# The diagonal products of a state-space scan in four column quarters of the array instead of two halves

## The chip, the cores and the metric

The kernel runs on one core of one Trainium2 chip. A core has TensorE (PE in the profile, with its weight loads listed apart as PEld), VectorE (DVE), ScalarE (ACT), GpSimd (POOL) and SyncE (SP, which issues most DMAs). The metric is the device time of one execution in microseconds, lower is better; times are medians of several runs.

## The reference

A batch of 32 sequences of 512 tokens and 256 channels goes through one block: a layer norm, a projection with rotary embedding, a gated state-space layer (scan) with 8 heads of 64 channels and a state of 128, an output projection, and then a mixture of experts (a shared part and 16 small experts, four of them chosen per token). The change touches one term of the scan:

```python
Acs = jnp.cumsum(Adt, axis=-1)
Lmat = jnp.exp(segsum(Adt))
Y_diag = jnp.einsum('bcln,bcsn,bhcls,bcshp->bclhp', Cr, Br, Lmat, xdt)
...
Y_off = jnp.einsum('bcln,bchpn,bhcl->bclhp', Cr, states_prev, jnp.exp(Acs))
return (Y_diag + Y_off).reshape(b, l, h, p)
```

`Y_diag` is the part of a token's output that comes from tokens of its own chunk. `l` is the query token, `s` the key token, `h` the head, `p` the channel in the head. Everything is float32.

## The kernel before

The kernel makes its own chunks of 128 tokens, four per sequence. For a chunk `c` and a head `h`, the decay times `C.B` stands in the tile `seg` as a matrix of 128 key tokens (partitions) by 128 query tokens, and the inputs in `xdt` as 128 key tokens by 64 channels of each of 8 heads. `diagonal(c)` (from L1567 of the source; its matmuls carry the line L1577 in the profile) multiplies them into one PSUM bank of the group `apb`: query tokens on partitions, 8 x 64 channels along the row. The stationary operand (the weights that are loaded) is a piece of `seg`, the moving operand the 64 columns of `xdt` that belong to the head. The loop over `n` cuts the 128 query tokens into two halves of 64, so each product uses 64 of the array's 128 columns, and the half's place in the PSUM partitions (0 or 64) is the column half of the array that it uses. That makes 16 matmuls for a chunk. A float32 matmul shows in the trace as two passes, each a weight load and a matmul record, so a chunk shows 32 loads and 32 matmuls. Over 32 sequences of 4 chunks there are 128 such chunks, 4096 records of each kind.

Large projections (helper `split_mm`, line L1443) run in another type (fp32r) with the operands split into a high and a low part, three products for one; their weights have 128 columns. Transposes have the lines L1452 and L1462, the state products L1560 and L1567 (float32, 512 moving columns, two passes), the router's L1492 and L1494 (16 or 32 moving columns), the products of B and C L1547, the cumulated decays L1518 to L1520 (the last with a weight of 32 columns), the down projection of the experts L1631.

Each engine runs one instruction list written out by hand. PE's is `lead`, `first`, `iteration(False)`, then a hardware loop of 29 repeats of `iteration`, then `tail`, `drain`, `last`. In `iteration` the work of three sequences is interleaved: the scan of one, the expert layer of the one before, the input projection of the next. The four `diagonal` calls stand between projections, each after others' work; PE waits for `m_ready` (DVE has multiplied `seg`, L1167) and for a free bank, and gives the bank to DVE's `chunk_y` (L1191, L1193). At the head of each repeat PE waits at L1530 for `hTl`, which DVE makes last in the repeat before. The loop's own jump has the line L1735.

Of the kernel before, what the change touches and what calls it, by code (L numbers as in the profile page):

```python
# [12 lines left out]
P = 128  # L13
# [19 lines left out]
def build(nc, x, wq_t, wzx_t, conv_w, conv_b, dt_bias, a_log, d_param, npw, ngw, wo_t,  # L33
# [6 lines left out]
    with ctx:  # L40
# [1366 lines left out]
        def _(pe):  # L1407
# [9 lines left out]
            def slot(name):  # L1417

                part, n = way.plan.where[name]
                w = len(BANKS[part])  # L1420
                if n >= w:
                    s, k = out_of(way.plan.slots[part][n - w][0], way.plan)
                    pe.wait_ge(sem[s], now(s, k) if SEM[s][3] else k)
                elif part != "p":
                    old = way.before if part in way.before.slots else way.plan
                    s, k = out_of([slot[0] for slot in old.slots[part][n::w]][-1], old)
                    pe.wait_ge(sem[s], k)
                return way.bank(name)

            def read_out(name):  # L1430
                s, k = out_of(name, way.plan)
                pe.wait_ge(sem[s], now(s, k) if SEM[s][3] else k)

            def fill(name, ins):
                part, n = way.plan.where[name]
                ins.then_inc(sem[f"{part}_for_{way.plan.slots[part][n][1]}"], 1)
# [132 lines left out]
            def diagonal(c):  # L1569
                b = slot(f"yd{c}")  # L1570
                read_out(f"xt{c}")
                pe.wait_ge(sem["m_ready"], c + 1)
                for h in range(HS):
                    hs = slice(h * PD, (h + 1) * PD)
                    for n in range(2):
                        ls = slice(n * P // 2, (n + 1) * P // 2)
                        ins = nc.tensor.matmul(b[ls, hs], seg[:, c % 2, h, ls], xdt[:, c % 2, hs], start=True, stop=True)  # L1577
                fill(f"yd{c}", ins)

# [81 lines left out]
            def first():  # L1661
                begin("first", "pa")
                consts(); weights_split(1, 2); project_z(0, 0); project_z(0, 1); project_z(1, 0)
                project_z(2, 0); project_z(1, 1); project_z(3, 0); project_x(4); project_x(5); project_x(0)
                project_z(2, 1); project_x(1); cumulate(); project_x(2); settled("ad_ready"); project_x(3)
                project_z(3, 1); x_by_token(0); CB(); x_by_token(1); B_by_token(); state(0); diagonal(0)
                state(1); from_state(1); diagonal(1); x_by_token(2); from_state(2); state(2); x_by_channel(0)
                y_by_channel(0); diagonal(2); x_by_token(3); weights_split(3); project_out(0)
                settled("a_out_ACT", "xdec_ready"); y_by_channel(1); project_q(0); project_out(1)
                from_state(3); y_by_channel(2); x_by_channel(1); diagonal(3); project_q(1); settled("xn_ready")  # L1670
                settled("m_ready"); project_out(2); settled("p_out_DVE"); y_by_channel(3); h_by_channel(0)
                project_out(3); settled("p_out_ACT"); settled("a_out_DVE", "yg_ready"); h_by_channel(1)
                settled("qn_ready")
                weights_split(*range(4, len(SPLIT)))
                assert not open_
# [117 lines left out]
```

## Time and profile before

| What | Value |
|---|---|
| Median of 3 runs | 3132.39 us (3128.45 to 3133.99) |
| The profiled execution's own time | 3137.47 us |
| Its span, first to last instruction | 3135.8 us |
| PE busy | 3058.7 us, 98% |
| PEld busy | 2624.5 us, 84% |
| DVE / POOL / ACT busy | 2360.5 / 2041.9 / 1934.2 us |
| The 29 repeats of the loop | about 94.4 to 94.9 us each |

The busy time of PE is that of records whose ends are modelled and which overlap, so it says that PE had work almost all the time, not how fast it went. For PE the distance from the start of one record to the start of the next of its kind is what is read. The pieces that the chain of waits gives to PE are such distances.

### The profile page before, as it was taken

The page shows a single profiled execution, that of the slowest core. Times are in us where ns is not written, and L with a number is a line of the kernel's source. Part 1 is how long each engine was busy: PE and PEld are TensorE (multiplying, and loading weights), DVE is VectorE, ACT ScalarE, POOL GpSimd, SP SyncE. Part 2 cuts the span into 40 slices and gives each one's busy share as a digit, 9 for nine tenths or more (in the row PEclk, how much of TensorE's full clock was granted, in tenths as well). Part 3 has the DMA queues.
Part 4 walks back from the last instruction along what each step waited for, and adds up shares of the span by engine and source line. Part 5 has one row for each costly group of instructions (what it writes and reads, how often), then busy time and mean ns, then how long its engine had stood idle before and what let it go on. Part 6 is the DMA issues. An engine that isn't in the chain of part 4 may idle for free.

```text
span 3135.8 us, 66479 instructions
## 1 busy us (share of the span) xinstructions
PE 3058.7 (98%) x21696; PEld 2624.5 (84%) x21696; DVE 2360.5 (75%) x5104; ACT 1934.2 (62%) x4149; POOL 2041.9 (65%) x2311
## 2 busy tenths in 40 slices
PE   5799999999999999999999999999999999999997
PEld 4688888888888888888888888888888888888876
DVE  5877877777777777777777777777777778777762
ACT  5566666666666566666666666666666666656562
POOL 2477666677666677666677666776666776666774
PEclk8899999999999999999999999999999999999998
DMA  3123222222222222222222222222222122222221
GB/s 125 41 69 89 74 76 66 67 67 88 74 65 69 70 72 81 78 68 61 73 78 78 81 67 58 67 87 78 78 66 62 67 88 74 81 61 67 68 82 41
DMA packets 143435, 227.37 MB, mean 73 GB/s; under 512 B 18976, under 2 KB 88352, under 8 KB 143392
## 3 DMA queue, kind: packets, MB, share of 16 engines
q1 hardware_dynamic: 126496, 210.06, 20.4%
q0 software_dynamic: 16896, 16.78, 4.1%
q8 instruction: 22, 0.36, 0.0%
q14 instruction: 21, 0.17, 0.0%
HBM read 174.87 MB, written 35.13 MB: 67 GB/s over the span
## 4 chain that ended last, share of the span: by engine, by line
PE 68%; POOL 24%; issue 2%; DMA 1%; DVE 1%; ACT 0%; POOLq 0%; SPq 0%; DVEq 0%; ACTq 0%
PE fpb L1443 25%; PE apb L1443 16%; PE acc L1631 13%; POOL hidL L652 5%; POOL hid L647 5%; POOL xD L622 3%; PE apb L1452 3%; PE apb L1577 2%; POOL zs L623 2%; PE apb L1567 2%; POOL rstd L583 1%; PE apb L1560 1%; PE ppb L1443 1%; POOL qrot L596 1%; POOL seg L607 1%
## 5 line engine op out<-in xcount | busy, mean ns | idle before, releaser
L652 POOL TENSOR_TENSOR hidL<-hid,hidH 128x512 fp32r<-128x512 f32 x384 | 546.2, 1422 | 239.3 <-ACT hidH L914 231.5
L1130 DVE SCALAR_TENSOR_TENSOR xc<-apb,cw,xc 128x511 f32<-128x511 f32 (+2 forms) x576 | 427.9, 747 | 70.3 <-ACT xc L827 42.1
L1631 PE MATMUL acc<-WDH,hidH 128*128 128x256 f32 x1536 | 458.2, 298 | 5.5 <-POOLq L654 4.7
L914 ACT CAST hidH<-hid 128x512 fp32r<-128x512 f32 x384 | 236.5, 616 | 368.2 <-POOL hid L647 310.2
L1631 PE MATMUL acc<-WDH,hidL 128*128 128x256 f32 x1536 | 432.3, 281 | 0.0
L1631 PE MATMUL acc<-WDL,hidH 128*128 128x256 f32 x1536 | 431.6, 281 | 0.0
L647 POOL TENSOR_TENSOR hid<-hid,cb 128x512 f32<-128x512 f32 x256 | 348.2, 1360 | 38.0 <-DMA cb<-c_row 13.4
L1249 DVE TENSOR_TENSOR hid<-hid,fpb 128x512 f32<-128x512 f32 x384 | 261.1, 680 | 142.4 <-PE fpb L1443 138.9
L1443 PE MATMUL fpb<-fTh,UH 128*128 128x512 f32 x768 | 336.4, 438 | 0.0
L1443 PE MATMUL fpb<-fTh,GH 128*128 128x512 f32 x768 | 319.5, 416 | 0.0
L845 ACT ACTIVATE seg<-seg,acs 128x128 f32<-128x128 f32 x1024 | 313.6, 389 | 8.9 <-ACT cb L895 5.7
L1631 PEld LDWEIGHTS acc<-WDH,hidH 128*128 128x128 f32 x1536 | 290.3, 189 | 26.7 <-POOLq L654 10.8
L1443 PE MATMUL fpb<-fTh,GL 128*128 128x512 f32 x768 | 304.8, 397 | 0.0
L1443 PE MATMUL fpb<-fTh,UL 128*128 128x512 f32 x768 | 303.8, 396 | 0.0
L1443 PE MATMUL fpb<-fTl,GH 128*128 128x512 f32 x768 | 303.7, 395 | 0.0
L1443 PE MATMUL fpb<-fTl,UH 128*128 128x512 f32 x768 | 302.5, 394 | 0.0
L1631 PEld LDWEIGHTS acc<-WDL,hidH 128*128 128x128 f32 x1536 | 290.8, 189 | 12.8 <-issue 7.2
L903 ACT ACTIVATE hid<-fpb 128x512 f32<-128x512 f32 x384 | 228.9, 596 | 115.5 <-PE fpb L1443 75.4
L1631 PEld LDWEIGHTS acc<-WDH,hidL 128*128 128x128 f32 x1536 | 290.2, 189 | 0.0
L622 POOL TENSOR_TENSOR xD<-xD,xdt 128x512 f32<-128x512 f32 x128 | 209.4, 1636 | 23.5 <-DVEq L1196 23.4
L827 ACT ACTIVATE xc<-apb,cbv,cw 128x512 f32<-128x512 f32 x192 | 149.2, 777 | 112.2 <-PE apb L1443 68.4
L1167 DVE TENSOR_TENSOR seg<-seg,CBs 128x1024 f32<-128x1024 f32 x128 | 166.0, 1297 | 43.1 <-ACT seg L845 33.6
(195 smaller groups left out, 8604.4 us busy)
## 6 DMA issues: line engine op xcount, KB each, us to landing
seg<-acs_row SPq DMA_DIRECT2D x128, 512.0 KB, 4.2
cb<-c_row SPq DMA_DIRECT2D x512, 128.0 KB, 2.9
xsP<-in_x SPq DMA_DIRECT2D x32, 512.0 KB, 3.7
xc<-qrot SPq DMA_DIRECT2D x32, 512.0 KB, 3.4
xc<-in_x SPq DMA_DIRECT2D x32, 512.0 KB, 4.4
out<-xc SPq DMA_DIRECT2D x32, 512.0 KB, 2.9
out<-xn POOLq DMA_DIRECT2D x32, 512.0 KB, 6.0
ZL_loaded<-in_wzx_t SPq DMA_DIRECT2D x2, 512.0 KB, 4.5
```

The lines of the kernel that those rows point to most:

```text
L622: own.do(G.tensor_tensor(xD[:, c % 2, :], xD[:, c % 2, :], xdt[:, c % 2, :], ALU.add))
L647: G.tensor_tensor(hid[:, j % 2, :], hid[:, j % 2, :], cb[:, r % 2, :], ALU.mult).then_inc(sem["routed_ready"], 1)
L652: own.do(G.tensor_tensor(hidL[:, j % 2, :], hid[:, j % 2, :], hidH[:, j % 2, :].bitcast(fp32), ALU.subtract))
L827: A.activation(xc[:, b, :], way.bank(f"xc{b}")[:], ACT.Identity, bias=cbv[:, b:b + 1], scale=cw[:, b, TAPS - 1:TAPS]).then_inc(sem["conv_f ...
L845: ins = A.activation(seg[:, c % 2, h, :], seg[:, c % 2, h, :], ACT.Exp, bias=acs[:, 0, c * HS + h:c * HS + h + 1])
L903: own.do(A.activation(hid[:, j % 2, :], way.bank(f"G{j}")[:], ACT.Silu))
L914: A.copy(hidH[:, j % 2, :], hid[:, j % 2, :]).then_inc(sem["hidden_high"], 1)
L1130: ins = V.scalar_tensor_tensor(xc[:, b, s:], src[:, 0:T - s], cw[:, b, TAPS - 1 - s:TAPS - s], xc[:, b, s:], ALU.mult, ALU.add)
L1167: V.tensor_tensor(seg[:, c % 2, :, :], seg[:, c % 2, :, :], CBs[:, c, :].unsqueeze(1).broadcast_to([P, HS, P]), ALU.mult).then_inc(sem["m_ ...
L1249: own.do(V.tensor_tensor(hid[:, j % 2, :], hid[:, j % 2, :], way.bank(f"U{j}")[:], ALU.mult))
L1443: ins = nc.tensor.matmul(dst, l, r, start=n == 0, stop=n == total - 1)
L1631: ins = nc.tensor.matmul(dst, l[:, w, tk], r[:, j, :], start=j == 0 and t % 2 == 0 and n == 0, stop=j == HB - 1 and n == 2, skip_group_che ...
```

## The change

The loop over halves becomes a loop over quarters of 32 query tokens. The moving operand stays at 64 columns, and the weights of one product have 32 columns instead of 64. A chunk has 32 matmuls instead of 16, in the trace 64 loads and 64 matmul records instead of 32, and each goes to one of four column quarters of the array (PSUM partitions 0, 32, 64, 96). Semaphores, banks and all other engines' lists are as before.

```diff
                 for h in range(HS):
                     hs = slice(h * PD, (h + 1) * PD)
-                    for n in range(2):
-                        ls = slice(n * P // 2, (n + 1) * P // 2)
+                    for n in range(4):
+                        ls = slice(n * P // 4, (n + 1) * P // 4)
                         ins = nc.tensor.matmul(b[ls, hs], seg[:, c % 2, h, ls], xdt[:, c % 2, hs], start=True, stop=True)
                 fill(f"yd{c}", ins)
```

On PE, at the first of the four chunks in the loop's repeat (`project_z(3, 1); diagonal(0); up(5)`), the list changes as follows (weights' columns x moving columns, then the count):

```order
 L1443 MATMUL apb<-ZL,hTh 128x256
 L1443 MATMUL apb<-ZH,hTl 128x256
-L1577 MATMUL apb<-xdt,seg 64x64 x16
+L1577 MATMUL apb<-xdt,seg 32x64 x32
 L1443 MATMUL fpb<-fTh,UH 128x512
 L1443 MATMUL fpb<-fTl,UH 128x512
```

Nothing else stands in another place: the block has twice as many instructions, between the same neighbours.

On PE, at the third chunk of the repeat (`up(7)`, `diagonal(2)`, then the transposes of `x_by_token(3)` and `down(5)`):

```order
 L1443 MATMUL fpb<-fTl,UH 128x512
 L1443 MATMUL fpb<-fTh,UL 128x512
-L1577 MATMUL apb<-xdt,seg 64x64 x16
+L1577 MATMUL apb<-xdt,seg 32x64 x32
 L1452 MATMUL apb<-ident,xc 128x128 x4
 L1631 MATMUL acc<-WDH,hidH 128x256
```

Here too the block grows in place. Counted in the built programs, one repeat of the loop on PE has 1,414 instructions before and 1,670 with the change, and the loop begins after 2,250 instructions before and after 2,762 with the change.

## Rows read from the trace of the kernel before

**Rows 1.** The page: engines' busy time, share of the span, and instructions.

```profile
PE 3058.7 (98%) x21696; PEld 2624.5 (84%) x21696; DVE 2360.5 (75%) x5104; ACT 1934.2 (62%) x4149; POOL 2041.9 (65%) x2311
```

**Rows 2.** Stretches: us, then each engine's busy us (instructions), granted clock, DMA share, GB/s.

```profile
174.00:2919.00 2745.00, 2742.86 (x19664) 2361.36 (x19663) 2117.32 (x4612) 1732.94 (x3742) 1846.92 (x2089) 1.00 0.25 73
1499.18:1594.03 94.85, 94.75 (x680) 81.43 (x679) 73.00 (x159) 59.83 (x130) 63.56 (x73) 1.00 0.24 72
```

**Rows 3.** Matmuls of L1577, all run: count, duration ns min/median/max, first and last start.

```profile
L1577 PE MATMUL apb<-xdt,seg x4096: 222/222/369, 70.4 to 3034.7; 128*64 128x64 f32 x196
```

**Rows 4.** Timeline of PE, 1504.5 to 1507: start us, us to its end, line, count.

```profile
1504.81 0.39 PE L1443 MATMUL fpb<-fTl,UH 128*128 128x512 f32 x1
1505.04 0.40 PE L1443 MATMUL fpb<-fTh,UL 128*128 128x512 f32 x1
1505.37 1.15 PE L1577 MATMUL apb<-xdt,seg 128*64 128x64 f32 x32
1506.45 0.66 PE L1452 MATMUL apb<-ident,xc 128*128 128x128 f32 x4
```

**Rows 5.** The same timeline in 1505.3 to 1505.42, the block's first records.

```profile
1505.37 0.14 PEld L1577 LDWEIGHTS apb<-xdt,seg 128*64 128x64 f32 x2 [0.37 <-issue]
1505.37 0.28 PE L1577 MATMUL apb<-xdt,seg 128*64 128x64 f32 x2
```

**Rows 6.** The chain of waits, 1640 to 1690: start us, us of the piece, line, count.

```profile
1644.44 0.10 PE fpb L1494
1644.55 0.12 PE fpb L1492
...
1667.24 0.89 PE apb L1547 x8
...
1671.37 0.44 PE apb L1452 x4
1671.81 0.44 PE fpb L1610 x4
...
1676.47 0.86 PE apb L1567 x2
```

**Rows 7.** Weight loads by line and form: count, busy us, mean ns, idle us before them.

```profile
L1577 PEld LDWEIGHTS apb<-xdt,seg 128*64 128x64 f32 x4096 | 130.4, 138 | 38.4 <-issue 34.3
...
L1567 PEld LDWEIGHTS apb<-xdec,Btok 128*128 128x128 f32 x192 | 36.2, 191 | 24.0 <-ACT zs L855 7.4 <-issue 6.9 <-DVE xD L1162 2.2
...
L1610 PEld LDWEIGHTS fpb<-ident,gt 128*16 128x16 f32 x128 | 11.4, 90 | 1.9
...
L1520 PEld LDWEIGHTS apb<-upper,ad 128*32 128x32 f32 x64 | 4.4, 108 | 1.3
```

**Rows 8.** DMA queues, 0 to 300 us: packets, MB, share of 16 engines.

```profile
q8 instruction: 14, 0.23, 0.3%
```

**Rows 9.** DMA queues, 300 to 2960 us (every queue that moved anything).

```profile
q1 hardware_dynamic: 103368, 178.51, 20.4%
q0 software_dynamic: 14784, 14.68, 4.2%
q14 instruction: 2, 0.02, 0.0%
```

**Rows 10.** The page: DMA queue 8 over the whole run, columns as in rows 8.

```profile
q8 instruction: 22, 0.36, 0.0%
```

**Rows 11.** PE's sequencer at the loop's jump: count, duration ns min/median/max, first and last start.

```profile
L1735 PEldq COMPARE_BRANCH  x29: 76/208/232, 306.3 to 2956.9; - x29
```

**Rows 12.** PE's sequencer at the first wait of a repeat, the same columns.

```profile
L1530 PEldq EVENT_SEMAPHORE  x32: 51/1968/2242, 34.2 to 2957.0; - x32
```

**Rows 13.** DMA issues by line, all run: count, size, median us from issue to landing.

```profile
acs_row<-acsT SPq DMA_DIRECT2D x32, 16.0 KB, 1.4
...
npwc<-in_npw SPq DMA_DIRECT2D x1, 1.0 KB, 3.1
...
ngwc<-in_ngw SPq DMA_DIRECT2D x1, 2.0 KB, 2.2
```

## The prediction

> **What bounds the kernel now.** I read the page's busy shares first [rows 1]: PE has work 98% of the span. Busy PE is not fast PE, so next the stretches [rows 2]: in the 2745 us that hold nearly all the repeats, PE is without work for 2.1 us, at a granted clock of 1.00 (the 2.4 GHz level), and the next busiest engine, DVE, is busy for 2117. One repeat takes 94.4 to 94.9 us and holds 680 matmul records and as many loads. So in the loop PE's own list sets the time. What PE's list gains or loses in a diagonal block moves the end by as much; other engines only follow, as they are released by PE. All that matters is how long PE stays in the block.
>
> The timeline of one block [rows 4] gives that. The 32 matmul records begin at 1505.37 and end 1.15 us later; the last one lasts 0.222 us [rows 3], so first to last start is 0.93 us. The next work starts at 1506.45, 1.08 us after the block began. At both edges there is a loss of about 0.1 us: the projection matmul before starts at 1505.04 and should be followed after 0.23 us, as it followed its neighbour, and not after 0.33; and the last product needs some 0.05 us, yet the next load is 0.15 us behind it. The array changes its partition there, and it will with quarters as with halves, so I leave the edges alone.
>
> **What limits a step of the block.** Two loads, of which one alone takes nearly as long (0.138 us, below), are over 0.14 us after the first began, and two matmuls are beside them [rows 5]: the two start less than 0.01 us apart, so both halves of the array work at once: 16 pairs in 0.93 us, 58 ns for a pair. What is 58 ns? A float32 pass over 512 columns takes 0.43 us (two in 0.86 [rows 6]), 0.84 ns a column, so 64 columns stream in 54 ns; 32 of them one behind the other would need 1.7 us, which confirms two at a time. Four transposes of 128 columns take 0.44 us, with 128-column weights as with 16-column weights (L1452 and L1610 [rows 6]): 110 ns where the stream is 107.5, so a stream-bound step is stream plus 2 to 3 ns, here 56 ns. The load is the other candidate: the router's records, with 16 or 32 moving columns, still take 0.22 us for two (L1494, L1492 [rows 6]), 0.11 us for a load of 128 columns, and half of that is 55 ns, and the B.C products with load and stream equal are 0.89/8 = 111 ns. So the pair's 58 ns is load-bound by a hair: load (55) plus a handshake of some 3 ns, with the stream only 2 ns behind.
>
> **The change part by part.** Each quarter sees the same 16 passes, 8 heads by two, that each half saw. The total of records doubles, and if four run at once the number of steps stays 16.
> - Step length. A 32-column load takes half, about 28 ns: the records' durations fall from 138 ns at 64 columns to 108 at 32 [rows 7]. The load leaves the step's bound; the moving operand still has 64 columns, so the stream stays at 56 ns. Gain 15 steps x 2 ns = 30 ns.
> - First load. It is not covered by a stream: 138 - 108 = 30 ns less [rows 7].
> - Four starts instead of two. The two of a pair start less than 10 ns apart [rows 5]; I take 7 ns for each further quarter, 14 ns lost in a block.
> - Sum: -46 ns. The bounds inside this mechanism are -60 ns (no loss for further starts), and, if those starts come back in every step, 16 x 14 = 224 ns less the 30 for the first load, some +0.19 us.
>
> With 128 blocks (4096/32 [rows 3]) that is 128 x -0.046 = -5.9 us, bounds -7.7 and +25 us. Against the profiled execution, whose own time is 3137.47 us with a span of 3135.8, it gives 3131.6; its distance to the median of 3132.39 is 5 us, a matter of that one execution, so by the median 3126.5. So a halved load buys nearly nothing, because a stream of the same length stands right behind it. The change moves the block from load-bound to stream-bound with 2 ns between the two.
>
> **The hidden part: PE's code.** 32 more loads and 32 more matmuls in each of four blocks are 256 more instructions in a repeat, 1,670 for 1,414. PE's code comes over queue 8 in packets of 16 KB (0.23 MB in 14 packets), all before 300 us [rows 8]; from 300 to 2960 us, 28 returns of the loop, queue 8 moves nothing [rows 9]. So today a repeat stays on the core. 256 instructions fill a packet (the 5,689 of the whole built program are 22 packets [rows 10]), so the loop lies from packet 8.8 to 14.3, touching 7; with the change from 10.8 to 17.3, touching 8, and the one fetched ahead makes 9. If only 8 are held, the packet with the loop's head is gone at the jump [rows 11] and must be fetched in each repeat. Cover: right after the jump PE's sequencer waits 1.97 us for DVE [rows 12], while the array works off its queue. A fetch shorter than that costs nothing. The nearest rows are a landing of 1.4 us for 16 KB, 2.2 us for 2 KB and 3.1 us for 1 KB [rows 13], so the price is between 0 and (3.1 - 2.0) x 29 = 33 us; 2.2 us would give 6 us. I take the 16 KB row, which is nearest in size, and so about nothing: 0.5 us in the forecast. **Forecast 3127 us.**
>
> The Trainium skill speaks against the change here: "Runtime: NRT & Kernel Launch", section on instruction fetch mechanics, gives PE 128 KiB, 2048 instructions in blocks of 16 KiB, and says that a taken branch to a block that is not resident forces a fetch before execution goes on. By it, 8 blocks are held and the fetch comes in every repeat; the rows agree that at least 8 are held, and no run here shows whether more are.
>
> **The rivals.**
> *Two at a time (0.10), the slower side.* The two passes of one product stand next to each other in PE's list on the same part of the array. To have four quarters at work, PE must look past the second pass of the first three. Before, it looked past one only. If that is as far as it sees, 64 records run in pairs: 32 steps of 56 to 58 ns are 1.79 to 1.86 us for 0.93, +0.86 to +0.93 us a block, +110 to +119 us: about 3245. For it: no row shows more than two parts of the array at work. Against it: the pairs already overtake without any loss, from the first record on [rows 5]. It decides as soon as a third part has to wait for a second pass.
>
> *A floor under the starts (0.08).* If PE can't start a matmul more often than the 29 ns it shows (0.93 us over 32), 64 records take 1.86 us, +119 us; any floor above 14 ns costs something, and at half that distance from 29 (22 ns) it is +0.48 us a block, +61 us. For it: each record brings a load too, and 128 instructions must be issued in 0.9 us, 7 ns each, for 15 now. Against it: two starts lie within 0.01 us of each other [rows 5].
>
> "TensorE: Matmul & The Clock Gate" of the Trainium skill, part 1, puts the start-to-start floor at about 25 ns however small the matmul; by that, 64 x 25 = 1.6 us, an estimate of +86 us. Its part 3 says that matmuls on different parts of the array start about 4 ns apart, which is nearer to what the pair shows.
>
> *The code is fetched and the fetch is seen (0.20).* As above, with landings over 2.0 us: +6 to +33 us, 3132 to 3159, likeliest near 3138.
>
> *More gain than I see (0.07).* The edges shrink, or the streams of four quarters need less than 54 ns: at 0.05 us more per block, -6 us more, about 3120. No row asks for it.
>
> **How the numbers follow.** Forecast (four at a time, fetch hidden or absent) 0.55, spread 3122 to 3132. A measurement of this kernel tells 0.2%, 6.3 us, from no change, so faster begins at 3126.1 and slower at 3138.7. The forecast's time lies 1 us inside "same": I put 0.23 of its 0.55 on faster, 0.32 on same. Visible fetch: 0.10 same, 0.10 slower. Two at a time and the floor: slower. More gain: faster. Faster 0.30, same 0.42, slower 0.28. The range leaves out the two rivals of +60 us and more (0.18) and holds the rest: 3116 to 3158.
>
> **What would show it.** Right: in the new timeline a block of 64 records with about 0.88 us between first and last start, the next load about 1.03 us after the first, the weight loads at about 108 ns, and all other lines at their old lengths. Two at a time or a floor: 1.6 to 1.9 us for the block, repeats longer by about 3.5 us. Fetch: packets on queue 8 between 320 and 2960 us, some 29 or more, and PE idle at the head of repeats, at L1443 behind L1530. The prediction is wrong in its ground if PE starts to wait for another engine inside the repeat, or if the edges of the block change.

## The result

| | before | after |
|---|---|---|
| median of the timed runs | 3131.39 us | 3299.91 us |
| lowest to highest | 3128.45 to 3133.99 | 3292.26 to 3304.44 |
| ratio, 95% interval | | 1.0536, 1.0510 to 1.0561 |
| span of the profiled execution | 3135.8 us | 3302.2 us |

The quarters cost 168.5 us where I had forecast 5 us gained, and the time lies far outside the range. The block itself came out as forecast; what happens at the loop's jump did not.

**The page of after** (engine busy, share, instructions; then the queue that carries code, against [rows 1, 10]):

```profile
PE 3107.5 (94%) x25792; PEld 2666.7 (81%) x25792; DVE 2369.1 (72%) x5104; ACT 1931.2 (58%) x4149; POOL 2033.6 (62%) x2311
...
q8 instruction: 278, 4.55, 0.6%
```

PE's share falls from 98% to 94%, and queue 8 moves 278 packets of code for 22. The extra packets come in the loop: of one repeat (1513.5 to 1613.2) the DMA view says

```profile
q8 instruction: 9, 0.15, 0.6%
```

where [rows 9] had nothing in 28 repeats. 9 x 28 = 252, and 252 + 26 for the longer program gives the 278.

**PE's sequencer at the loop's jump** (count, ns min/median/max, first and last start; [rows 11] before):

```profile
L1735 PEldq COMPARE_BRANCH  x29: 76/3747/4072, 307.9 to 3122.2; - x29
```

One return takes 3.7 us for 0.21. First to last start over 28 gives the mean repeat: 100.51 us, for 94.66 in [rows 11]. The difference times 28 is 164 of the 168.5 us.

**The timeline of PE over one jump**, which begins at 1513.5 and takes 3.40 us (start us, us to its end, line; in brackets how long PE was idle and what ended it):

```profile
1515.11 0.40 PE L1443 MATMUL fpb<-fTl,UH 128*128 128x512 f32 x1
1515.35 0.39 PE L1443 MATMUL fpb<-fTh,UL 128*128 128x512 f32 x1
1517.07 0.36 PE L1443 MATMUL apb<-ZH,hTh 128*128 128x264 f32 x1 [1.33 <-PEq L1530]
1517.27 0.28 PE L1443 MATMUL apb<-ZL,hTh 128*128 128x264 f32 x1
1520.07 0.28 PE L1443 MATMUL apb<-ZH,hTl 128*128 128x264 f32 x1 [2.51 <-issue]
1520.19 0.28 PE L1443 MATMUL apb<-ZH,hTh 128*128 128x264 f32 x1
...
1520.56 0.40 PE L1443 MATMUL apb<-ZH,hTh 128*128 128x264 f32 x1
1520.75 0.42 PE L1443 MATMUL apb<-ZL,hTh 128*128 128x264 f32 x1
1520.97 0.42 PE L1443 MATMUL apb<-ZH,hTl 128*128 128x264 f32 x1
```

Read it from the top. The array works off what the sequencer had sent ahead, until about 1515.6, so 2.1 of the 3.4 us are hidden. Then it is idle for 1.33 us. Two matmuls come, and it is idle again for 2.51 us, "issue": nothing that another engine owes. And from 1520.56 on the same matmuls start 0.22 us apart for 0.12. The stretches show why (us, busy us of PE, PEld, DVE, ACT, POOL with instructions, granted clock, DMA share, GB/s; [rows 2] before):

```profile
174.00:2919.00 2745.00, 2633.10 (x22137) 2267.94 (x22126) 2006.90 (x4350) 1632.76 (x3537) 1746.97 (x1982) 0.98 0.24 70
1513.50:1613.20 99.70, 95.85 (x807) 82.52 (x806) 73.30 (x160) 59.71 (x129) 63.58 (x73) 0.98 0.24 71
1517.55:1520.05 2.50, 0.00 (x1) 0.00 (x0) 0.00 (x0) 1.42 (x3) 2.24 (x3) 1.00 0.02 7
1520.60:1523.60 3.00, 3.00 (x14) 2.81 (x14) 0.33 (x2) 0.00 (x0) 0.62 (x1) 0.50 0.02 5
1523.60:1613.20 89.60, 89.60 (x778) 77.24 (x777) 70.39 (x151) 55.32 (x121) 56.42 (x63) 1.00 0.25 71
```

After the two idle stretches the granted clock is 0.50 (1.2 GHz) before it is 1.00 (2.4 GHz) again, in this repeat as in each of the others, for 3.4 us (15 repeats) or 6.8 us (13). So a repeat pays three times. On average over the 28, PE is idle for 1.66 us at the jump (1.26 to 2.00; the repeat shown is one of the mildest) and for 2.62 us at the second stop (2.26 to 2.89). Without its idle time a repeat takes 95.75 us with the shorter low stretch and 96.77 with the longer one, where quarters_half_moved of experiment 1 takes 94.16 at a clock of 1.00: the low clock costs 1.6 or 2.6 us, 2.06 on average. Against the 94.66 us of before, 0.5 us come back: 0.2 in the blocks, 0.16 at the down projection of experiment 4 (0.03 us in every repeat for a mean of 0.19), and a rest for which no single row stands. 1.66 + 2.62 + 2.06 - 0.5 is the 5.85 us.

**One block** in the timeline, and its records by duration (against [rows 4, 3, 7]):

```profile
1564.92 0.28 PE L1443 MATMUL apb<-ZH,hTl 128*128 128x256 f32 x1
1565.13 1.10 PE L1577 MATMUL apb<-xdt,seg 128*32 128x64 f32 x64
1566.16 0.51 PE L1443 MATMUL fpb<-fTh,UH 128*128 128x512 f32 x1
```

```profile
L1577 PEld LDWEIGHTS apb<-xdt,seg x8192: 106/110/178, 72.2 to 3200.3; 128*32 128x32 f32 x200
L1577 PE MATMUL apb<-xdt,seg x8192: 216/219/317, 72.2 to 3200.3; 128*32 128x64 f32 x200
```

64 records in 1.10 - 0.22 = 0.88 us from the first start to the last, and the next work 1.03 us behind the first: four quarters run at a time, and a block is 0.05 us shorter (over the 112 blocks of the loop 1031 ns to the next work, for 1082).

### The profile page after: what moved, and what is told of

Read it like the earlier page. It is cut to its first block and busy times, and to the rows that moved or that the text cites. A ratio compares the mean times of both kernels' runs of the same rounds, so it can differ in the third digit from the quotient of the medians.

```text
span 3302.2 us, 74671 instructions
## 1 busy us (share of the span) xinstructions
PE 3107.5 (94%) x25792; PEld 2666.7 (81%) x25792; DVE 2369.1 (72%) x5104; ACT 1931.2 (58%) x4149; POOL 2033.6 (62%) x2311
## 5 line engine op out<-in xcount | busy, mean ns | idle before, releaser
L1443 PE MATMUL fpb<-fTh,UH 128*128 128x512 f32 x768 | 336.3, 438 | 0.0
L1443 PE MATMUL fpb<-fTh,GH 128*128 128x512 f32 x768 | 319.3, 416 | 0.0
L1443 PE MATMUL fpb<-fTh,GL 128*128 128x512 f32 x768 | 304.9, 397 | 0.0
L1443 PE MATMUL fpb<-fTl,GH 128*128 128x512 f32 x768 | 303.9, 396 | 0.0
L1443 PE MATMUL fpb<-fTh,UL 128*128 128x512 f32 x768 | 303.5, 395 | 0.0
L1443 PE MATMUL fpb<-fTl,UH 128*128 128x512 f32 x768 | 303.3, 395 | 0.0
L1443 PEld LDWEIGHTS apb<-ZH,hTh 128*128 128x128 f32 x512 | 108.3, 211 | 155.3 <-issue 148.1
```

Source lines behind the costliest of these rows:

```text
L1443: ins = nc.tensor.matmul(dst, l, r, start=n == 0, stop=n == total - 1)
```

## The experiments

A packet is 256 instructions of PE's list, and a border is where one packet ends and the next begins. The theory from here on: PE holds 8 packets of code, one of them read ahead. A loop that touches 7 stays; one that touches 8 needs 9 and loses its head before it comes back. Rivals: the quarters themselves disturb PE (twice the records), or 1,670 instructions are too many wherever they lie. All ratios are against the kernel before on the same chip; it takes 3127.88 to 3131.39 us on all of them but that of experiment 6, so times of experiments 1 to 5 can be set beside each other to within some 3 us.

### 1. The loop moved by 128 and by 64 instructions

```diff
-            def diagonal(c):
+            def diagonal(c, parts=4):
...
-                    for n in range(4):
-                        ls = slice(n * P // 4, (n + 1) * P // 4)
+                    for n in range(parts):
+                        ls = slice(n * P // parts, (n + 1) * P // parts)
...                                     # in first(), ahead of the loop
-                ... state(0); diagonal(0)
-                state(1); from_state(1); diagonal(1); ...
+                ... state(0); diagonal(0, 2)
+                state(1); from_state(1); diagonal(1, 2); ...
```

quarters_half_moved has the first of these two calls alone.

> Two of the four diagonal blocks that stand ahead of the loop (those of the first pass, of 128) keep halves; all others, and the whole loop, are as in the changed kernel. The loop keeps its 1,670 instructions, but starts 128 earlier in PE's list: packets 10.29 to 16.81 of PE's code, 7 of them, where the changed kernel has 10.79 to 17.31, 8 of them. Theory 'the loop no longer stays on the core' (room for 8 packets, one of them fetched ahead): nothing on queue 8 after about 300 us, a return of the loop of about 210 ns for 3,500, repeats of 94.3 us, and the whole at 126 x 51 ns under before: about 3125 us, ratio 0.998. Rival 'the quarters themselves' (twice the records, four parts of the array, slow the repeat and lower the clock): about 3300 us as before the move, with or without packets. Rival 'too many instructions' (a loop of 1,670 isn't held wherever it lies): about 3300 us, 9 packets a repeat.

Measured: 3128.34 us, ratio 0.9992 (0.9979 to 1.0005), 25 packets on queue 8 in the whole run. The loop is the one of the changed kernel, instruction for instruction; 128 instructions fewer ahead of it take 172 us away. Both rivals fall: neither the quarters nor the length of 1,670 costs anything here. But the 6 us of the blocks are not there; experiments 4 to 6 look for them.

> One of the blocks ahead of the loop keeps halves: the loop lies from packet 10.54 to 17.06, so it touches 8 again, but its head is now 118 instructions ahead of the next packet's border, for 54 in the changed kernel. Theory 'the loop no longer stays on the core': 9 packets a repeat; the return of the loop still takes about 3.5 us (net +1.4 to +1.9 us a repeat, 28 times: +40 to +53 us); the second stall of 2.8 us goes, since the next packet has 118 instructions' time to land. If the granted clock then stays at 1.00: about 3170 us; if the first stall alone lowers it (+1.3 to +2.5 us a repeat): 3210 to 3240. Rivals 'the quarters themselves' and 'too many instructions': 3300 us, no difference by the place.

Measured: 3174.74 us, 1.0147 (1.0132 to 1.0163), 278 packets. Its jump, the timeline behind one, and the stretch of that repeat:

```profile
L1735 PEldq COMPARE_BRANCH  x29: 76/3542/4067, 302.9 to 2990.9; - x29
```

```profile
1457.02 0.39 PE L1443 MATMUL fpb<-fTh,UL 128*128 128x512 f32 x1
1458.81 0.36 PE L1443 MATMUL apb<-ZH,hTh 128*128 128x264 f32 x1 [1.40 <-PEq L1530]
1459.01 0.28 PE L1443 MATMUL apb<-ZL,hTh 128*128 128x264 f32 x1
1459.13 0.29 PE L1443 MATMUL apb<-ZH,hTl 128*128 128x264 f32 x1
```

```profile
1455.15:1550.63 95.48, 94.08 (x807) 80.98 (x806) 71.89 (x160) 59.89 (x129) 62.74 (x73) 1.00 0.26 73
```

The return is as slow as in the changed kernel, the second stop is gone, and the matmuls go on 0.12 us apart: the granted clock is 1.00 (it falls in 4 of the 28 repeats, where the idle stretch is 1.8 to 2.0 us; others of that length leave it). So the price splits: 45 us for the fetch at the jump, and the other 125 us of the changed kernel for the second stop (2.62 us x 28 = 73 us) and for the half clock that comes with it (some 52 us). The first stop alone seldom brings the clock down.

### 2. Halves with a long loop

```diff
+        s_idle = ctx.enter_context(nc.semaphore("nobody_waits"))
...
-            def split_mm(dst, parts, read=None):
+            def split_mm(dst, parts, read=None, idle=0):
...
                         n += 1
+                        for k in range(idle * (n - 1) // total, idle * n // total):
+                            pe.sem_inc(s_idle, 1 - 2 * (k % 2))
...                                     # hidden(): idle=10, project_z(): idle=2
...                                     # halves_long_moved alone, at the head of lead():
+                for k in range(96):
+                    pe.sem_inc(s_idle, 1 - 2 * (k % 2))
```

> The kernel before, halves as they were, with 256 more instructions in PE's repeat that do nothing: increments and decrements of a semaphore that nobody waits for, 10 in each gate and up projection and 2 in each z projection, between their matmuls. The loop then has 1,670 instructions from packet 9.85 to 16.38, touching 8. Theory 'the loop no longer stays on the core': 9 packets a repeat, the return at about 3.5 us, the second stall, repeats of about 100 us: some 3290 to 3300 us with no quarter in it. Rival 'the quarters themselves': 3132 us and no packets. Rival 'too many instructions': 3300 us.

> As halves_long, with 96 more of the same empty instructions at the very start of PE's list, where PE waits for its first data: the loop of 1,670 instructions lies from packet 10.23 to 16.75, touching 7. Theory 'the loop no longer stays on the core': no packets after 300 us, 3132 us, at most 5 us more for what the empty instructions cost between matmuls that are longer than they. Rival 'too many instructions': 3300 us. If the empty instructions themselves were what costs in halves_long: 3300 us too, without packets.

Measured: halves_long 3130.76 us, 1.0001 (0.9992 to 1.0011), 26 packets, none in the loop; halves_long_moved 3134.39 us, 1.0017 (1.0007 to 1.0026), as expected. The first is a miss for my own theory, and it would have kept "the quarters themselves" alive had quarters_moved not been fast. The fault was in my count. The changed kernel's second stop comes between instructions 2768 and 2769, 7 into its loop (the trace shows a wait, three weight loads and two matmuls ahead of it), and a stop for the next packet can only stand at a border; by my count the next border was 2816. If every border lies 47 instructions earlier (give or take one; what runs ahead of the program's own list no trace shows), the loops touch

| kernel | loop's first instruction | in packets, borders 47 earlier | touched | fetched in a repeat |
|---|---|---|---|---|
| before | 2250 | 8.97 to 14.50 | 7 | 0 |
| after | 2762 | 10.97 to 17.50 | 8 | 9 |
| quarters_moved | 2634 | 10.47 to 17.00 | 7 | 0 |
| quarters_half_moved | 2698 | 10.72 to 17.25 | 8 | 9 |
| halves_long | 2522 | 10.04 to 16.56 | 7 | 0 |
| halves_long_moved | 2618 | 10.41 to 16.93 | 7 | 0 |

which fits all six (quarters_half_moved then has 71 instructions from its head to the border, the changed kernel 7). The table was made to fit, so it needed a test of its own.

### 3. Sixteen instructions, in both directions

```diff
 # halves_long_back: no empty instructions in the z projections of first()
-    ... else None, idle=2))
+    ... else None, idle=2 * (way.plan is not PLANS["first"])))
 # quarters_16: the changed kernel, at the head of lead()
+                for k in range(16):
+                    pe.sem_inc(s_idle, 1 - 2 * (k % 2))
```

> halves_long without the 16 empty instructions in the z projections of the first pass, which stand ahead of the loop; the loop itself is the same. It starts at instruction 2506 for 2522. Why: by my count from the first instruction halves_long touched 8 packets and was not fetched again, which the theory did not allow. But in the changed kernel the second stall comes after 7 instructions of the loop, and my count has 54 to the next border. If the borders lie 47 instructions earlier than I counted (theory 'borders at -47'), halves_long has its head 9 instructions behind a border and touches 7 packets, as before does; quarters_moved and halves_long_moved touch 7; the changed kernel and quarters_half_moved 8. By it, these 16 instructions fewer put the head 7 ahead of a border, as in the changed kernel: 8 packets touched, 9 fetched in each repeat, the long return, the second stall, repeats of about 100 us, and some 3295 us. Rival 'the quarters themselves are needed for it' (their records, or the pace at which they take instructions): 3131 us like halves_long, no packets in the loop.

> The changed kernel with all its quarters and 16 empty instructions at the very start of PE's list, where PE waits for its first data. The loop starts at 2778 for 2762. 'Borders at -47': the head is 9 instructions behind a border for 7 ahead of one, 7 packets touched, nothing fetched after some 310 us, about 3128 us as quarters_moved. If the borders lay at multiples of 256 as I first counted, 8 packets would be touched still (10.85 to 17.38): about 3300 us. 'The quarters themselves': 3300 us.

Measured: halves_long_back 3352.67 us, 1.0716 (1.0699 to 1.0732), 278 packets; quarters_16 3126.58 us, 0.9989 (0.9980 to 0.9998), 26 packets. The jump of halves_long, of halves_long_back and of quarters_16:

```profile
L1738 PEldq COMPARE_BRANCH  x29: 76/208/237, 310.2 to 2955.3; - x29
```

```profile
L1738 PEldq COMPARE_BRANCH  x29: 76/4097/4387, 307.3 to 3176.2; - x29
```

```profile
L1738 PEldq COMPARE_BRANCH  x29: 76/208/237, 305.5 to 2955.7; - x29
```

Taking 16 empty instructions away ahead of a loop of halves adds 222 us; putting 16 ahead of the loop of quarters removes 173. The border is where the second stop says it is, to 16 instructions, and neither the quarters nor the loop's 1,670 instructions cost anything by themselves. One number is off: I expected 3295 for halves_long_back. Its timeline (jump at 1537.4):

```profile
1537.81 0.40 PE L1444 MATMUL fpb<-fTh,UL 128*128 128x512 f32 x1
1541.65 0.39 PE L1444 MATMUL apb<-ZH,hTh 128*128 128x264 f32 x1 [3.44 <-PEq L1533]
1541.85 0.41 PE L1444 MATMUL apb<-ZL,hTh 128*128 128x264 f32 x1
1544.60 0.38 PE L1444 MATMUL apb<-ZH,hTl 128*128 128x264 f32 x1 [2.33 <-issue]
```

At the jump the array had two matmuls left, some 0.6 us of work, where the changed kernel had 2.1, so 3.44 us of the return are bare for 1.33. Over the 28 repeats the mean is 3.58 us for 1.66. The second stop is 0.28 us shorter (2.34 for 2.62), and the rest of a repeat 0.3 us longer: its blocks are halves, 0.2 us more, and the low clock lasts 6.8 us in every repeat. Together that is 1.95 us a repeat, 55 us in all, nearly the 53 us that lie between this run and the changed kernel. That the empty instructions between the last matmuls keep the sequencer from running ahead is the likely reason, not a shown one.

### 4. Where the blocks' 6 us went: a later down projection

With the code resident, each block is still 51 ns shorter, 0.20 us a repeat, yet the mean repeat of quarters_16 is (2955.7 - 305.5)/28 = 94.65 us, for 94.66. The view of waits, PE's weight loads at down(10) (total us, times, longest), before and in quarters_16:

```profile
PEld acc L1631 <- POOLq L654: 10.8, 20, 3.0
```

```profile
PEld acc L1632 <- POOLq L655: 15.4, 35, 2.9
```

From the last transpose ahead of it to down(10)'s first matmul it is 0.31 us in every repeat, for POOL's remainder of block 10; before, 0.32 us in 15 of the 28 repeats and 0.03 in the others, a mean of 0.19. So 0.12 of the 0.20 us stand there; where the other 0.08 went, no single row shows. The timelines of POOL and DVE in the kernel before, in a repeat with the wait and in one without:

```profile
873.94 0.51 POOL L582 TENSOR_SCALAR ve<-mv 128x2 f32<-128x2 f32 x1
874.53 0.82 POOL L583 TENSOR_TENSOR rstd<-ve,mhalf 128x2 f32<-128x2 f32 x1
...
968.58 0.19 POOL L582 TENSOR_SCALAR ve<-mv 128x2 f32<-128x2 f32 x1
968.86 0.95 POOL L583 TENSOR_TENSOR rstd<-ve,mhalf 128x2 f32<-128x2 f32 x1
```

```profile
873.92 0.87 DVE L1219 SCALAR_TENSOR_TENSOR xc<-xc,rstd 128x256 f32<-128x256 f32 x2
...
968.78 0.87 DVE L1219 SCALAR_TENSOR_TENSOR xc<-xc,rstd 128x256 f32<-128x256 f32 x2
```

POOL's L582 that starts 0.02 us behind DVE's L1219 takes 0.51 us for 0.19; one that starts 0.20 us ahead of it is through. The Trainium skill, "SBUF — State Buffer", section "Who interferes with whom", says that DVE and GpSimd share a pair of ports, and that the one that issues second waits for the first. The rows agree (an L582 that starts 0.010 to 0.013 us behind, as in 6 repeats, still takes 0.19). In the kernel before, L582 takes 0.51 us ahead of just the 15 repeats that wait; in quarters_16 it does ahead of all 28.

First try, PE's list (on quarters_moved, and on the kernel before):

```diff
-                if g: down(10)
-                settled("ffn_in_ready"); project_z(2, 0); project_x(5)
+                settled("ffn_in_ready"); project_z(2, 0)
+                if g: down(10)
+                project_x(5)
```

> quarters_moved with one more step: in the loop, PE makes the down projection of block 10 after the z projection of token tile 2 and not ahead of it, 1.4 us later. Why: quarters_moved is only 1.2 us under before, though each of its blocks is 51 ns shorter, 0.2 us a repeat. In its trace PE's down(10) waits 0.31 us for POOL's hidL (L652) in every repeat, for 0.03 to 0.33 us (mean 0.19) in the kernel before, so the gain seems to have turned into this wait. Theory 'POOL's chain to down(10) is late, PE has 0.2 us a repeat to give': without the wait the repeat falls to 94.25 us, 28 x 0.4 us less than quarters_moved: 3115 to 3119 us, ratio 0.996. Rival 'another engine's round sets the repeat at 94.65 us': the wait appears at the next place, 3128 us.

> The kernel before with the same step alone: down(10) behind the z projection of token tile 2, halves as they were. Theory 'POOL's chain is late': the waits of 0.35 us in about half the repeats go, 94.45 us in all, 3123 to 3125 us; the difference between this and the same with quarters is then what the blocks give, 126 x 51 ns = 6.4 us. Rival: no change, 3130 us.

Measured: quarters_down 3167.75 us, 1.0123 (1.0108 to 1.0139); halves_down 3168.77, 1.0125 (1.0109 to 1.0140). Both misses. The projection that went ahead now stands for its bank, which ACT still has to read out (waits, quarters_down):

```profile
PE apb L1443 <- ACT zs L855: 46.8, 30, 1.6
```

1.6 us in every repeat (1.2 in halves_down). The experiment tells nothing of the blocks.

### 5. POOL's remainder first

```diff
-                combine(11); rest(10); rest(11)
+                rest(10); combine(11); rest(11)
```

> quarters_16 with one swap in POOL's list of the loop: the remainder of hidden block 10 (hidL, which PE's down(10) waits for) is made ahead of the product of block 11 and not behind it. Why: in quarters_16 PE waits 0.31 us for POOL at down(10) in every repeat; in the kernel before it waits so in about half of them, and those are the repeats in which POOL's L582 takes 0.51 us for 0.19 (it starts 0.70 us ahead of the jump, not 0.88). So the blocks' 0.2 us a repeat went into POOL's lateness. POOL's chain has ACT's hidH(10) at hand 1.2 us before it makes hidL(10), so the swap lets PE off. Theory 'POOL's lateness ate the gain': no wait at down(10), repeats of 94.25 us, 28 x 0.4 = 11 us under quarters_16 and 0.2 us x 28 more than the same swap gives the kernel before: 3114 to 3119 us, ratio 0.996. Rival 'something else holds the repeat at 94.65 us': the wait turns up elsewhere (at down(11), 1.3 us later, or at a bank), 3127 us or more.

> The kernel before with the same swap in POOL's list, halves as they were. Theory 'POOL's lateness': the waits of about half the repeats go, repeats of 94.45 us, 3123 to 3125 us, ratio 0.998; the difference to quarters_16_rest is what the blocks give, some 6 us. Rival: the wait turns up elsewhere, 3130 us.

Measured: quarters_16_rest 3208.16 us, 1.0254 (1.0240 to 1.0268); halves_rest 3218.89, 1.0290 (1.0276 to 1.0304). The wait at down(10) is gone, as expected, but the rival's case came, harder than I had put it. ACT's row of halves_rest, and PE's wait:

```profile
1387.67 0.62 ACT L914 CAST hidH<-hid 128x512 fp32r<-128x512 f32 x1 [2.07 <-POOL hid L647]
```

```profile
PE apb L1443 <- ACT zs L855: 59.0, 31, 2.0
```

Block 11's product is late, ACT stands 2.07 us for it, and the z tile behind it on ACT keeps its bank. Part of the price is the clock again: in 14 of the 28 repeats of halves_rest the granted clock is 0.50 for 3.4 us after this wait, and these take 98.16 us for 96.59, 22 of the 91 us. As in experiment 4, a step moved by some 1.3 us held up the next step in the same engine's list.

### 6. The same steps in another order

```diff
-                G.tensor_scalar(shift[:, ts], moments[:, ts, 0], -1.0, 0.0, ALU.mult, ALU.add)
                 own.do(G.tensor_scalar(var[:, ts], moments[:, ts, 1], 1.0, EPS, ALU.mult, ALU.add))
-                own.do(G.tensor_tensor(scale[:, ts], var[:, ts], mhalf[:, ts], ALU.pow))
+                G.tensor_tensor(scale[:, ts], var[:, ts], mhalf[:, ts], ALU.pow)
+                own.do(G.tensor_scalar(shift[:, ts], moments[:, ts, 0], -1.0, 0.0, ALU.mult, ALU.add))
```

> quarters_16 with POOL's four small steps of each norm in another order: variance, power, negated mean, product, for negated mean, variance, power, product. Why: the swap of the runs before took PE's wait at down(10) away, but put block 11's product late, and PE then stood 2 us for ACT. In the trace POOL is late at down(10) in just those repeats in which the variance step (L582) starts behind DVE's L1219 and takes 0.51 us for 0.19; in the others it is done 0.2 us earlier and the power takes 0.95 us for 0.82. With the variance first it starts 0.25 us earlier, ahead of DVE's instruction; the power takes 0.95, and the negation follows: some 1.76 us to the product step for 1.95. Theory 'POOL's lateness ate the gain': the wait at down(10) falls from 0.31 to about 0.1 us, nothing else moves, repeats of some 94.4 us: 3119 to 3123 us, ratio 0.997. Rival 'the order makes no difference, POOL meets DVE anyway': 0.31 us still, 3127 us.

> The kernel before with the same order of POOL's small steps, halves as they were. Theory 'POOL's lateness': the waits of 0.33 us in half the repeats go, 94.45 to 94.5 us: 3124 to 3126 us, ratio 0.9985; quarters_16_terms is then 3 to 6 us under it, the blocks' gain as far as POOL lets it through. Rival: 3129 us, no change.

Measured, on a chip where the kernel before takes 3139.75 us: quarters_16_terms 3130.49, 0.9970 (0.9956 to 0.9984); halves_terms 3128.26, 0.9961 (0.9947 to 0.9974). Their jumps:

```profile
L1738 PEldq COMPARE_BRANCH  x29: 76/208/237, 306.1 to 2952.1; - x29
```

```profile
L1735 PEldq COMPARE_BRANCH  x29: 76/208/237, 304.9 to 2949.2; - x29
```

94.50 us a repeat with quarters, 94.44 with halves, for 94.66 in the kernel before. With POOL's new order the wait of the kernel with halves is gone in every repeat. The ratio of 0.4% is more than that: the loop gives (94.66 - 94.44) x 28 = 6 of the 11.5 us, the kernel before has no trace on this chip, and there its runs scatter from 3133 to 3146 us. With quarters 0.14 us of interval at down(10) are left where 0.03 is no wait. So POOL's lateness did eat most of the blocks' gain, but the second half of what I expected (quarters 3 to 6 us under halves) did not come: as soon as PE has 0.2 us less to do, it meets POOL again. From 35 to 5 us ahead of the jump that ends a repeat of quarters_16, POOL is busy for over 9 of 10 us (the last column of busy time; columns as above):

```profile
1501.40:1511.40 10.00, 10.00 (x119) 8.38 (x119) 8.39 (x12) 8.23 (x19) 9.44 (x8) 1.00 0.40 133
1511.40:1521.40 10.00, 10.00 (x129) 8.97 (x128) 6.51 (x15) 3.83 (x11) 9.14 (x12) 1.00 0.18 44
1521.40:1531.40 10.00, 10.00 (x70) 9.18 (x69) 7.94 (x17) 4.46 (x11) 9.39 (x11) 1.00 0.15 44
```

Which of POOL's steps there sets the new limit was not tried. Of the two kernels with the new order, the one without any quarter has the shorter repeat.

## Why the prediction was wrong

- **The block: right.** Forecast 0.884 us from first to last start and 46 ns saved; measured 0.88 and 51 ns. Four quarters run at a time, and the edge behind the block stays (149 ns from the last start to the next work, for 152). That the load leaves the bound is argued from this agreement; no run lengthened the load or the stream alone. "Two at a time" and "a floor under the starts" are out.
- **The code: seen, and priced wrong.** The term that failed is "A fetch shorter than that costs nothing ... I take the 16 KB row, which is nearest in size, and so about nothing: 0.5 us in the forecast". The cover was sized well for this kernel (2.1 us of queued work, for 1.97 us). The fetch was not: the branch takes 3.3 to 4.1 us. In the trace the packet starts 1.0 us after the branch (median; 0.9 to 1.7), takes 1.2 us (0.9 to 1.7), and PE goes on 1.4 us after its end (1.3 to 1.6); the landing row of 1.4 us stood for the whole of this. Alone it is 45 us (quarters_half_moved), where the forecast had 0.5 and the rival at most 33.
- **A second stop that no case held.** I priced one packet a repeat. The jump lands in a packet that is gone, and the next one is gone as well; the head stands 7 instructions ahead of that border, not 54 as by the prediction's count from the list's first instruction, so nothing covers its fetch, which starts 0.7 us (median) after the branch is done: 2.6 us of idle PE a repeat, 73 us.
- **The clock.** After 1.3 to 2.0 us and again 2.3 to 2.9 us of idle time PE is granted 1.2 GHz for 3.4 or 6.8 us, 2.06 us a repeat, 58 us. No case held it.
- **The chances.** The profile showed that a loop of 7 packets stays, and the count gives 8 after the change, 9 with the one read ahead. That the fetch comes in every repeat deserved most of the chance; I gave its visible form 0.20, though its sign came just as I had written it (packets on queue 8 in the loop, PE idle at L1443 behind L1530). The Trainium skill, "Runtime: NRT & Kernel Launch", section "Instruction fetch mechanics", gives PE 128 KiB in blocks of 16 KiB as a FIFO. The runs agree: 7 touched stay, 8 do not. The Trainium skill's condition there for the fetch at a taken branch is a target outside "the current 2-page window"; on PE the runs differ, for the kernel before jumps back over 7 packets and fetches none. The Trainium skill's sentence there that the cost of a border is mostly hidden agrees for the borders inside the loop and not for one 7 instructions behind a jump.
- **The gain that was left.** With the code resident the forecast's 3127 was met (quarters_16 3126.58), partly by luck: of the blocks' 204 ns a repeat at least 0.12 us went into a wait for POOL, which I had excluded ("other engines only follow"), and the mean repeat is 94.65 us for 94.66. The ratio of 0.9989 is no gain that this kernel's measurement tells well from none.

## What to carry to other kernels

Before lengthening the body of a loop, count the packets of 256 instructions that it touches on the engine that runs it, from a border that a trace shows (a stop shortly behind the jump, or the packets on the code queue); a body that just fits can be mended by a few instructions ahead of it. Price a fetch by the whole stop of the sequencer and not by the transfer, and ask what is fetched next and what the clock does after the idle time. An engine whose share of busy time is 65% can still be the one that the bottleneck meets at the seam of a repeat: look at its share in the stretch ahead of that seam.

## What the runs showed that I had not expected

- PE's code: a loop that touches 7 packets of 256 instructions (the longest here 1,670 instructions) moves nothing on queue 8; one of the same length that touches 8 fetches 9 in each repeat. 16 instructions decide between 3126.58 and 3299.91 us.
- A return to a packet that is gone stops PE's sequencer for 3.3 to 4.4 us, for 0.21.
- One idle stretch of 1.2 to 2.1 us in each repeat left the granted clock at 1.00 in 24 of 28 (quarters_half_moved), one of 1.2 to 1.6 us in all 28 (quarters_down); 1.3 to 2.0 us followed by 2.3 to 2.9 us brought 0.50 every time (the changed kernel).
- POOL's L582, a step of 0.19 us, takes 0.51 us when it starts 0.015 us behind DVE's L1219; that third of a microsecond goes with whether a repeat of the kernel before takes 94.5 or 94.8 us, in all 28.
